# Spacing 32 indirect stores by TensorE's progress in an attention and mixture-of-experts kernel

## The reference

```python
x = x.reshape(-1, 512)                                  # 2048 tokens
shared = silu(x @ sw_gate) * (x @ sw_up) @ sw_down      # sw_*: 512 x 1408, 1408 x 512
probs = softmax(x @ router_w.T)                         # 8 experts
top_w, top_i = top_k(probs, 2); top_w = top_w / top_w.sum(-1)
routed = sum over the two experts e of top_w[e] * (silu(x @ w_gate[e]) * (x @ w_up[e])) @ w_down[e]
out = x_in + routed + sigmoid(x @ shared_gate_w) * shared   # x: layer-normed x_in
```

## Time and profile before

| | |
|---|---|
| median of 3 runs | 939.79 us (939.73 to 942.89) |
| the profiled execution's own time | 942.02 us |
| its span, first to last instruction | 939.7 us |
| mean granted TensorE clock | 0.980 |
| PE busy | 876.7 us, 93% of the span |
| chain that ended last | PE 68%, ACT 1%, issue 1%, DVE 1%, DMA 0% |
| 32 indirect stores (L591) | 32.9 us busy on POOL, 408.1 to 450.5 us |

### The profile page before, as it was taken

One profiled execution on the slowest core, in us unless ns is written; L12 is line 12 of the kernel. 1 busy time (PEld: TensorE's weight loads), 2 busy tenths in 40 slices (PEclk: granted clock), 3 DMA queues, 4 the chain that ended last, 5 costly groups with the idle time before them and its releaser, 6 DMA issues.

```text
span 939.7 us, 14497 instructions
## 1 busy us (share of the span) xinstructions
PE 876.7 (93%) x4560; PEld 748.0 (80%) x4560; DVE 571.4 (61%) x920; ACT 518.9 (55%) x879; POOL 473.7 (50%) x460
## 2 busy tenths in 40 slices
PE   4899999899988999998899999999999999999993
PEld 3677777787767888886688888888899999999992
DVE  5788787878773642431121212112899999999892
ACT  4788888888765331120111211112688888888881
POOL 5787878787720000047100000000489999999984
PEclk9999999999999999999799999999999999999997
DMA  9344343525625322200032002552964444443542
GB/s 145 83 142 128 127 142 101 160 96 156 224 90 157 100 68 90 90 1 1 1 120 39 1 1 90 185 184 93 300 145 72 87 70 80 76 87 67 90 63 39
DMA packets 70142, 93.77 MB, mean 100 GB/s; under 512 B 16137, under 2 KB 35593, under 8 KB 70098
## 3 DMA queue, kind: packets, MB, share of 16 engines
q1 hardware_dynamic: 60338, 72.73, 25.9%
q0 software_dynamic: 9760, 20.49, 12.3%
HBM read 65.59 MB, written 27.60 MB: 99 GB/s over the span
## 4 chain that ended last, share of the span: by engine, by line
PE 68%; ACT 1%; issue 1%; DVE 1%; DMA 0%; POOLq 0%; SPq 0%; POOL 0%; DVEq 0%; ACTq 0%
PE bank L1347 9%; PE bank L1345 8%; PE bank L1346 8%; PE bank L1412 5%; PE bank L1414 5%; PE bank L1413 5%; PE bank L1359 4%; PE bank L1360 4%; PE bank L1361 4%; PE bank L1436 3%; PE bank L1437 3%; PE bank L1438 3%; PE bank L1369 2%; PE bank L1423 1%; DMA stg<-in_L_ffn_sw_down 0%
## 5 line engine op out<-in xcount | busy, mean ns | idle before, releaser
L1033 DVE TENSOR_TENSOR sg<-bank,sg 128x512 f32<-128x512 f32 x44 | 30.4, 692 | 224.0 <-PE bank L1347 187.5
L606 POOL DMA_INDIRECT xg<-x_normed_rows,meta x39 | 39.7, 1018 | 219.3 <-PE bank L1369 159.7
L1347 PE MATMUL bank<-x_hl,wsp 128*128 128x512 f32 x352 | 138.5, 393 | 5.2 <-issue 5.1
L1346 PE MATMUL bank<-x_hl,wsp 128*128 128x512 f32 x352 | 138.1, 392 | 2.3 <-issue 2.3
L1345 PE MATMUL bank<-x_hl,wsp 128*128 128x512 f32 x352 | 138.3, 393 | 0.7 <-issue 0.6
L785 ACT ACTIVATE sg<-bank 128x512 f32<-128x512 f32 x44 | 26.3, 597 | 164.9 <-PE bank L1347 147.8
L591 POOL DMA_INDIRECT slot_rows<-msrc,posi x32 | 32.9, 1030 | 135.9 <-DVE posi L1140 126.5
L685 ACT ACTIVATE pth<-bank 128x512 fp32r<-128x512 f32 x128 | 73.3, 598 | 45.8 <-PE bank L1239 43.9
L931 DVE TENSOR_TENSOR ptl<-bank,pth 128x512 fp32r<-128x512 f32 x128 | 86.0, 682 | 17.6 <-ACT pth L685 17.2
L792 ACT ACTIVATE hh<-sg 128x512 fp32r<-128x512 f32 x44 | 27.8, 631 | 123.7 <-DVE sg L1033 107.9
L548 POOL TENSOR_SCALAR pb<-pb,rinv 128x512 f32<-128x512 f32 x128 | 87.4, 696 | 13.3 <-DVE rinv L927 7.8
(11 more groups left out here) (157 smaller groups left out, 2353.9 us busy)
## 6 DMA issues: line engine op xcount, KB each, us to landing
cd<-in_ctx SPq DMA_DIRECT2D x32, 256.0 KB, 5.0
wex<-in_L_ffn_w_gate SPq DMA_DIRECT2D x8, 704.0 KB, 4.3
wex<-in_L_ffn_w_up SPq DMA_DIRECT2D x8, 704.0 KB, 5.7
xb<-in_x SPq DMA_DIRECT2D x16, 256.0 KB, 4.5
cn<-in_ctx SPq DMA_DIRECT2D x16, 256.0 KB, 3.0
x2b<-in_x SPq DMA_DIRECT2D x16, 256.0 KB, 2.8
x_rows<-x2b SPq DMA_DIRECT2D x16, 256.0 KB, 2.1
x_normed_rows<-x2n SPq DMA_DIRECT2D x16, 256.0 KB, 2.0
```

The lines of the kernel that those rows point to most:

```text
L1346: te.matmul(bk[:, :], hi, xlo, start=False, stop=False)
L1347: ins = te.matmul(bk[:, :], lo, xhi, start=False, stop=(h == HC - 1))
```

## The change

Before each of the 32 indirect stores POOL waits for e_u. Store number m = 2 t + k (0 to 31) waits until e_u is at least 16 + m // 3, that is until PE has ended `gate_up` of step n = 15 + m // 3. So three stores are let go after each of the steps (1, 4), (1, 5), ..., (2, 2), and the last two after (2, 3).

```diff
             g.wait_ge(st_meta0, 16)
             for t in range(NT):
                 for k in range(TOPK):
+
+                    g.wait_ge(e_u, SC + 5 + (TOPK * t + k) // 3)
                     g.indirect_dma_start(out=meta_d, out_offset=bass.IndirectOffsetOnAxis(ap=posi[:, t, k:k + 1], axis=0),
                                          in_=msrc[:, t, k, :], in_offset=None).then_inc(st_meta, 16)
```

## The result

| | kernel before | changed kernel |
|---|---|---|
| median | 939.96 us (939.71 to 943.52, 6 runs) | 927.02 us (923.49 to 931.45, 6 runs) |
| ratio of the runs | | 0.986 (95% interval 0.9836 to 0.9884) |
| profiled execution's own time | 942.02 us | 931.45 us |
| its span | 939.7 us | 929.1 us |
| mean granted TensorE clock | 0.980 | 0.985 |

The changed kernel is faster by 1.4%, 12.9 us between the medians. The forecast was 926.1 us, within 924.5 to 940.5.

What follows compares the result with a forecast made beforehand. PE was taken to bound the kernel, with 13.66 us lost in one stalled step. Waits and moved stores cost 0, so 942.02 - 13.66 = 928.4 us profiled, less 2.23 us: 926.1 us, range 924.5 to 940.5.

Steps and rivals of the forecast that it cites:

- What bounds the kernel: PE sets the end; one shared-layer step, 438.46 to 460.28 us, lost 13.66 us to issue pauses and a lower clock.
- The added waits: 32 waits added to POOL's list: between 0 and 9.9 us of POOL's time, none of it on the chain.
- The moved stores: Later stores on POOL, ending at about 495.4 us, delay table reload and first gather; cost 0, without cover 6 us.
- The cover: Time from the first gather, about 505 us, until PE wants its rows at 642.7 us: 138 us.
- The stall: PE's long step near 440 us goes when POOL's unbroken run of stores goes: -13.66 us, bounds -13.66 and 0.
- the far end: Of the bounds -13.66 and 0 for PE's long step, the choice of -13.66 us, the whole loss gone.
- the cover of 5.8 us: Between DVE's low part and PE's use of it: a signal may come 5.8 us late before PE sees it.
- The sum: Whole kernel: 942.02 - 13.66 = 928.4 us for a profiled execution, 926.1 us for the median.
- Not the density: PE's long step comes from the number of stores or something else at 420 to 453 us; 939.8 us, chance 0.17.
- Only when watched: PE's long step belongs to the profiled execution, so unwatched runs gain nothing; 939.8 us, chance 0.10.
- The burst hurts: Each store group beside ACT's and DVE's short chain costs PE 1.37 us per store; 969.8 us, chance 0.08.
- The rule weighed against the change: Skill text: a DMA's semaphore write costs about one cycle, so spacing POOL's stores changes nothing; 939.8 us.

Runs made afterwards that it cites:

- the later run: Against the changed kernel: all 32 stores in one unbroken run again, let go only after step (2, 6); 951.33 us, ratio 1.0089 to the kernel before.
- six a step: Against the changed kernel: six stores let go for each step in place of three; 927.25 us, ratio 0.9817 to the kernel before.
- paced: Against the changed kernel: six POOL clears between two stores replace the wait for PE; ratios to the kernel before 1.0000, 0.9976, and 0.986 where that stalled.
- two runs of 16: Against the changed kernel: stores in two unbroken runs of 16, the second five steps after the first's start; 930.69 us, ratio 0.9863 to the kernel before.
- the two kernels that would tell: Scratch indirect stores in a row, real stores later: positions in order, 928.96 us; 16 rows in place of 128, 930.62 us; kernel before 929.10.

## Why the prediction was right, and where it was lucky

**What bounds the kernel.** Right. PE set the end, and the 13.66 us of the one long step were on the chain: the medians differ by 12.9 us, and with the later run the loss in the profile and the timed runs both grew by 8.8 us.

**The added waits.** Right: 0. PE has no wait of the kind left, and POOL's idle time before a store whose wait is met is 0.30 us.

**The moved stores.** Right in shape. The profiled execution of the changed kernel reached step (1, 3) at 400.97 us where the earlier trace rows has 397.66, so everything is 3.3 us late against the working. With that, the last two stores at 496.61 us (493.2 + 3.3 = 496.5 forecast), SP's reload at 500.52 (497 + 3.3 = 500.3) and PE's first transposes of gathered rows at 645.94 (642.7 + 3.3 = 646.0) are as worked out. The first gather came 2 us sooner, at 506.27 (505 + 3.3 = 508.3), since from the reload's issue to it took 5.75 us in place of 7.9. The cover was 645.94 - 506.27 = 140 us; the forecast was 138.

**The stall.** The term was -13.66 us and the step that it stood for is gone. The choice of the far end was right with room to spare: six a step loses nothing either. That stores with rests between them do not stall PE is shown on chips that stall by three kernels (three a step, six a step, paced); two runs of 16 lost 1.3 us. Two readings behind the term were too kind. The first late signal was not DVE's, due at 427.89 us, but ACT's: its silu started at 426.85 where 416.94 + 8.16 = 425.10 was due, 17 us into the run:

```profile
416.94 0.60 ACT L785 ACTIVATE sg<-bank 128x512 f32<-128x512 f32 x1 [3.98 <-PE bank L1347]
...
426.85 0.60 ACT L785 ACTIVATE sg<-bank 128x512 f32<-128x512 f32 x1 [5.76 <-remote]
```

And the cover of 5.8 us counts one late signal, where two runs of 16 had three slow hand-overs in a row. With three stores a step no signal came late at all, so neither mattered.

**The sum.** 928.4 us was forecast for a profiled execution and 931.45 measured. The missing 3.1 us are the 3.3 us lost before step (1, 3), which the diff does not touch. Part of it lies in attention: from 23 to 46 us in the span the granted clock was 0.81, where the kernel before had 0.96. That stretch varies from trace to trace: DVE's multiply of step (1, 3), at 403.44 us before and 406.71 after, stands between 401.26 and 408.03 us in the fourteen traces. The median, 927.02, is 0.9 us above the forecast; with runs from 923.49 to 931.45 us, so near a hit is partly luck.

**The rivals.** "Not the density" had two halves. That something else near 440 us causes the stall fell with the later run, where it moved with the stores; that their number does fell with the changed kernel, six a step and the paced kernel, which do all 32. "Only when watched" fell with the result. "The burst hurts" fell too. DVE's multiply and low part take 0.69 us beside the bursts as elsewhere, though some stores are slowed, below.

**The rule weighed against the change.** By the Trainium skill ("DMA: Bandwidth & Descriptors", section Anatomy of one DMA) a semaphore write is nearly free, and the sum would have been 939.8 us. The time says otherwise, but the rule itself is not refuted: 32 plain DMAs with the same increments in 17 us cost PE nothing on a stalling chip, and whether the late signals come from the increments at all is not shown. The step from "increments are cheap" to "these stores cannot make signals late" is what did not hold.

**What the prediction did not see.** It took the stall for a property of the kernel. It is one of the kernel on some chips. Of the chips compared in the experiments, the kernel before took 942.5 and 942.6 us on two, and 929.1 and 930.7 on the other two. On those the step of the sum, -13.66 us, has nothing to take away. The changed kernel itself was not run on such a chip; its nearest kin there, the paced stores, gave ratios of 1.0000 and 0.9976 with 1 inside both intervals. The forecast was right because the profile that it was made from and the comparison that gave the result both came from chips on which it stalls, and that was luck: nothing in the prediction asked for it. If half of the chips are like the two without the stall, which four chips cannot tell, the gain over all chips is about half of 1.4%.

**Open.** Whether PE's signals and the indirect stores share a resource, and which, is not settled, nor what PE itself waited for in its "issue" pauses; a late supply of instructions to PE was not tested. Nor is whether it is the indirect way of issuing, the descriptor for each row or the scattered places in DRAM, since the two kernels that would tell ran where nothing stalls. The plain DMAs do not tell it either, as their run of 17 us ended where the late signals of the indirect stores only began. Nor what differs between the chips, or between what was loaded on them: each chip was compared on one occasion, so the chip and the occasion cannot be told apart.

## What to carry to other kernels

When an engine shows "issue" pauses and its partners are late with "remote" as the releaser, look for a neighbour that has issued small indirect DMAs without a rest, and give that neighbour a pace; here 1.5 us of rest after each store of 0.96 us, or three stores to 8.16 us, was enough, and the stores' consumer had 140 us of cover to pay for it. Both paces did the same here: prefer one that does not tie two engines together, or one that is tied to the engine that suffers if its own rate may change. And before a term of a sum rests on a stall that no dependence explains, time and profile the unchanged kernel on a second chip.

## What the runs showed of the hardware

- One program, two behaviours by chip: 32 indirect stores of 128 pieces of 8 bytes, one each 1.26 us, made TensorE's semaphore signals up to 17.9 us late and cost 13.66 us in the profile of the earlier trace rows, and in another one did nothing (steps of 8.16 us, signals on time to 0.03 us). The timed runs fall into the same two groups: 942.5 and 942.6 us on two chips, 929.1 and 930.7 us on two others. Placed later, the same stores made a signal 24.6 us late and cost 22.4 us.
- The lateness has a slow onset. On stalling chips the first signal to ACT that came over 1 us late was due 12.7 to 20.9 us into an unbroken run of stores (12.7 in the late run, 17.0 in the kernel before, 20.9 in the first run of 16 and with six a step), and DVE's first 15.5 to 23.7 us into it, and PE's signals came again within 6 us of the last store (561.10 + 0.96 to 567.58 us in the late run).
- A fall of the clock is the second part of such a stall. The granted clock was 0.63 on average in the step of 29.66 us, after PE had paused, and 0.89 in the next, which PE worked through without a wait. Of the 22.4 us lost in that run PE's pauses are 15.2; nearly all of the rest is slower matmuls, 0.43 us apart where 0.23 is usual.
- A store that starts while a DVE instruction with two inputs in SBUF is under way takes longer. In the changed kernel one at 440.76 us took 1.48 us in place of 0.96, beside the low part of 0.69 us that began at 440.71 and was not slowed:

```profile
440.71 0.69 DVE L1037 TENSOR_TENSOR hl<-sg,hh 128x512 fp32r<-128x512 f32 x1 [0.70 <-ACT hh L794]
```

  This agrees with the Trainium skill ("GPSIMD Engine Reference", section Key points), which says that GpSimd shares its SBUF interfaces with VectorE and meets it in instructions with two SBUF inputs. The store before it, at 439.49 us, started beside the multiply, which reads one input from PSUM, and took 0.96 us. The traces add the size: the extra time is what was left of the DVE instruction when the store started, less 0.12 or 0.13 us (0.52 us for 0.64 left here; 0.33 for 0.45 and 1.53 for 1.66 in the kernel before, at 431.50 and 422.39 us). A store that had begun first was not slowed (0.96 us at 545.95 in the late run, DVE's low part from 546.21).
